# Cross-attention and mixture-of-experts kernel on one core: the split expert weights move from 192 to 64 modulo 256 bytes in SBUF

## What is computed

```
x = x + xattn(ctx_1024, layernorm(x), ...)      # 16 heads of 64, 77 context rows per batch
h = layernorm(x)
probs  = softmax(h @ Wr)                        # 9 experts, the best 2 of a token, weights rescaled to sum 1
gate   = silu(einsum('th,ehi->tei', h, Wg))     # 256 -> 704
hidden = gate * einsum('th,ehi->tei', h, Wu)    # 256 -> 704
out    = einsum('tei,eih,te->th', hidden, Wd, cw)   # 704 -> 256
x = x + out
```

## Time and profile before

| | before |
|---|---|
| median of 3 runs | 799.77 us (799.15 to 800.23) |
| profiled execution, whole | 799.43 us |
| profiled execution, span | 797.6 us |
| PE busy in the span | 769.0 us (96%) |
| PEld busy | 736.7 us (92%) |
| DVE busy | 649.1 us (81%) |
| ACT busy | 609.9 us (76%) |
| granted TensorE clock, mean | 0.991 |

### The profile page before, as it was taken

The page is one execution under the profiler, slowest core; times in us unless marked ns, Lnnn a source line. Parts: engine busy times, 40 slices in busy tenths (PEclk is TensorE's granted clock), DMA queues, the critical chain, the costliest instruction groups (busy, mean ns, idle before and its releaser), DMA issues.

```text
span 797.6 us, 19771 instructions
## 1 busy us (share of the span) xinstructions
PE 769.0 (96%) x6057; PEld 736.7 (92%) x6057; DVE 649.1 (81%) x1584; ACT 609.9 (76%) x1942; POOL 389.4 (49%) x541
## 2 busy tenths in 40 slices
PE   9988999999999999998999999999999999999994
PEld 8857999999999999897999999999999999999994
DVE  6667898898888878887878888787897878879882
ACT  4869988898889888734877778787777877778772
POOL 5603676777777766752233243333324333234343
PEclk9999999999999999998999999999999999999998
DMA  8576401401401211645574463565656656473222
GB/s 309 162 189 208 129 28 43 146 28 41 146 29 42 80 35 38 203 134 154 148 220 99 110 167 81 125 147 147 167 153 166 154 142 169 96 217 81 49 26 28
DMA packets 78212, 96.40 MB, mean 121 GB/s; under 512 B 10851, under 2 KB 65307, under 8 KB 77979
## 3 DMA queue, kind: packets, MB, share of 16 engines
q1 hardware_dynamic: 64667, 77.25, 31.1%
q0 software_dynamic: 13440, 17.90, 12.7%
HBM read 109.46 MB, written 30.23 MB: 175 GB/s over the span
## 4 chain that ended last, share of the span: by engine, by line
PE 87%; DVE 4%; POOL 3%; issue 2%; ACT 2%; SPq 1%; DVEq 1%; DMA 1%; POOLq 0%; ACTq 0%
PE banks L362 25%; PE banks L363 24%; PE banks L364 24%; PE banks L1555 4%; PE banks L1721 2%; PE banks L1410 2%; PE banks L1569 2%; SPq L640 1%; PE banks L1494 1%; PE banks L1506 1%; DVEq L1774 1%; POOL expert_in L955 1%; POOL prob L984 1%; PE banks L1530 0%; PE banks L1693 0%
## 5 line engine op out<-in xcount | busy, mean ns | idle before, releaser
L362 PE MATMUL banks<-tok_t_hi,wgt_hi 128*128 128x256 f32 x704 | 201.4, 286 | 5.6 <-issue 4.3
L1046 POOL DMA_INDIRECT result<-res,tok_id x72 | 122.5, 1702 | 162.5 <-ACT res L1305 145.0
L363 PE MATMUL banks<-tok_t_lo,wgt_hi 128*128 128x256 f32 x704 | 196.8, 280 | 0.0
L364 PE MATMUL banks<-tok_t_hi,wgt_lo 128*128 128x256 f32 x704 | 196.8, 280 | 0.0
L1170 ACT ACTIVATE prob<-banks,row_min 128x77 f32<-128x77 f32 x512 | 161.4, 373 | 4.2 <-DVE row_min L1923 4.2
L362 PEld LDWEIGHTS banks<-tok_t_hi,wgt_hi 128*128 128x128 f32 x704 | 133.8, 190 | 7.6 <-issue 7.5
L363 PEld LDWEIGHTS banks<-tok_t_lo,wgt_hi 128*128 128x128 f32 x704 | 133.5, 190 | 0.0
L364 PEld LDWEIGHTS banks<-tok_t_hi,wgt_lo 128*128 128x128 f32 x704 | 133.2, 189 | 0.0
L1170 ACT ACTIVATION_READ_ACCUMULATOR prob<-banks,row_min 128x1 f32 x512 | 130.0, 256 | 0.0
L362 PE MATMUL banks<-wgt_hi,hid_hi 128*128 128x256 f32 x360 | 101.5, 282 | 0.7 <-DVE hid_hi L2239 0.7
L984 POOL TENSOR_TENSOR prob<-prob,row_inv 128x1232 f32<-128x1232 f32 x32 | 72.1, 2253 | 59.8 <-DVE row_inv L1937 59.8
(11 more groups left out here) (280 smaller groups left out, 2173.9 us busy)
## 6 DMA issues: line engine op xcount, KB each, us to landing
wgt<-in_L_ffn_Wg SPq DMA_DIRECT2D x29, 704.0 KB
wgt<-in_L_ffn_Wu SPq DMA_DIRECT2D x29, 640.0 KB
wgt<-in_L_ffn_Wd SPq DMA_DIRECT2D x29, 640.0 KB
tok<-expert_in SPq DMA_DIRECT2D x32, 258.0 KB, 3.8
spare_wgt<-in_L_ffn_Wg SPq DMA_DIRECT2D x9, 704.0 KB, 4.6
spare_wgt<-in_L_ffn_Wu SPq DMA_DIRECT2D x9, 640.0 KB, 5.9
spare_wgt<-in_L_ffn_Wd SPq DMA_DIRECT2D x9, 640.0 KB, 6.2
valmat_f<-valmat_dram SPq DMA_DIRECT2D x4, 1197.0 KB, 6.2
```

The lines of the kernel that those rows point to most:

```text
L362: nc.tensor.matmul(to, a[0], b[0], start=first, stop=False)
L363: nc.tensor.matmul(to, a[0], b[1], start=False, stop=False)
L364: return nc.tensor.matmul(to, a[1], b[0], start=False, stop=last)
L1046: nc.gpsimd.indirect_dma_start(out, bass.IndirectOffsetOnAxis(ap=tok_id[:, t % NOTES, a:a + 1], axis=0), res[i][:, a, :], None, compute_op ...
```

## The change

Two gap tensors grow from 16 to 48 columns of 4 bytes (+128 bytes each), and the third, of 32 columns (128 bytes), is gone.

```diff
-        sb("line_gap0", [P, 16], F32, ffn)
+        sb("line_gap0", [P, 48], F32, ffn)
         wgt_hi = [sb("wgt_hi0", [P, WCOLS], F32R, ffn)]
         wgt_lo = [sb("wgt_lo0", [P, WCOLS], F32R, ffn)]
         gate_act = [sb(f"gate_act{i}", [P, 2, W], F32, ffn) for i in range(2)]
         hid_f = [sb(f"hid_f{i}", [P, 2, W], F32, ffn) for i in range(2)]
-        sb("line_gap1", [P, 16], F32, ffn)
+        sb("line_gap1", [P, 48], F32, ffn)
         hid = [[sb("hid0_hi", [P, FC, W], F32R, ffn), sb("hid0_lo", [P, FC, W], F32R, ffn)],
                [sb("hid1_hi", [P, FC, W], F32R, ffn), hid1_lo]]
         res = [sb("res0", [P, WB, D], F32, ffn), res1]
...
         wgt = sb("wgt", [P, WEIGHT_SLOTS, WCOLS], F32, ffn)
-        sb("line_gap2", [P, 32], F32, ffn)
         wgt_hi.append(sb("wgt_hi1", [P, WCOLS], F32R, ffn))
```

## The result

| | before | after |
|---|---|---|
| median of the runs | 799.90 us (798.68 to 801.06, 6 runs) | 802.53 us (801.20 to 803.27, 6 runs) |
| ratio, 95% interval | | 1.0037 (1.0026 to 1.0048) |
| span of the profiled execution | 797.6 us | 799.8 us |

The change makes the kernel slower by 0.37%, 2.6 us at the medians. The page's head after it answers to the earlier trace rows: same instructions, PE busy for 4.4 us more.

What follows compares the result with a forecast made beforehand. PE's matmul pitch in the expert stage was taken as the bound. Matmuls +2.7 us and singles -0.6, with 0.4 hidden by pauses, gave +1.7 us: a median of 801.5 us, range 795.2 to 805.6.

Steps and rivals of the forecast that it cites:

- The bound: Expert stage: its length is PE's matmuls, read from the start-to-start pitch; PE busy 408.19 of 413 us.
- Step 1, the kind: Expert stage's gate_up and down: runs still settle at 113.5 or 117.9 ns, with somewhat more slow pitch; attention unchanged.
- Step 1, the size: Gate_up and down going from +64 to -64: an even mix of fast and slow pitch, 2.7 us more.
- half price: Lower bound for gate_up and down at -64, if a single tile's price counts by half: 1.1 us more.
- full price: Upper bound for gate_up and down at -64, if a single tile's price counts in full: 6.8 us more.
- That a run's beginning counts: Gate_up and down runs: position alone does not decide the pitch; it depends also on how the run begins.
- Step 2: Single tiles going to +64: their 96 long matmuls fall from 394 to 388 ns, giving back 0.6 us.
- Steps 3 and 4: DVE and ACT reading and writing from other places, and loads and stores moved by 128 or 256 bytes: nothing.
- The pauses: PE's eight waits at tile boundaries in the expert stage: hide about a fifth of the matmuls' loss, 0.4 us.
- The fast pitch as the rule: Rival: all gate_up and down fall to 113.5 ns, 795.9 us; faster in one form or another has chance 0.33.
- No effect: Rival: gate_up and down pitch comes from how a run begins, not the distance; time stays at 799.8 us; chance 0.25.
- The slow pitch as the rule: Rival: -64 puts all gate_up and down at 117.9 ns, +7.1 us, 806.9 us; chance 0.08.

Runs made afterwards that it cites:

- e12: e9's placing of parts, but around the change's distance of -64 instead of +64 between stationary and moving operands; 798.75 us, 0.9989 against the kernel before.
- e9: Kernel before, with gate and up columns of wgt_lo and both hid_lo 128 bytes apart from their rounded parts, wgt_lo's down rows level; 796.23 us, 0.9954.
- e1: Kernel before, with tokens, split weights and hidden rows all moved by 128 bytes, so every distance stays; 800.26 us, 1.0011.
- e2: Kernel before, with split weights and hidden rows moved and tokens left: gate_up gets the change's -64, down keeps its distances; 799.33 us, 0.9992.
- e3: Kernel before, with hid0_lo moved to 128 modulo 256, apart from hid0_hi, as slot 1 has it; 799.79 us, 1.0000.
- e4: Kernel before, with hid1_lo moved from 128 to 0 modulo 256, level with hid1_hi; 800.28 us, 1.0003.
- e8: Kernel before, with tokens, split weights and hidden rows all at 128 modulo 256, so every distance is 0; 810.01 us, 1.0122.
- e5: Kernel before, with wgt_lo0 alone moved from 192 to 64 modulo 256, apart from its rounded part in slot 0; 1.0003.
- e6: Kernel before, with wgt_lo apart from wgt_hi in both slots, hid_lo level in both, and three small tables moved into gaps; 1.0003.
- e7: As e6, with both hid_lo also 128 bytes apart from their hid_hi; 804.10 us, 1.0044 against the kernel before.
- e11: Kernel before, with only tok_t_lo, gate_up's moving rest, put 128 bytes apart from tok_t_hi; 802.86 us, 1.0025.

## Why the prediction was right, and where it was not

**The bound** was right. The time moved with PE's pitch: 4.1 + 0.25 - 1.7 = 2.65 us by the count, against 2.2 us between the profiled spans and 2.6 between the medians.

**Step 1, the kind.** Right: the two pitches are still there, the attention did not answer (318.20 against 317.86 us busy, with one matmul more in the stretch), and -64 has a larger share of the slow one. e12 against e9, and the eight runs that e1 and e2 tell apart, show that this is the distance and not this one arrangement.

**Step 1, the size.** It was too small: 4.1 us instead of 2.7. I had the share go from 0.30 to an even mix of 0.50; by the starts it went from 0.39 to 0.69. Two things were off. The even mix was a choice for want of evidence; the measured 4.1 us lie about midway between its half price (1.1 us) and its full price (6.8 us). And I read the share from mean durations, which understated it before (0.28 and 0.34), and gave "means near 279.5" as the sign of the size. The mean was 279 (whole stage, line 363), as forecast, but it says little, for durations do not keep to the pitch. These are the groups of 48 gate_up matmuls at the slow pitch (388.8 to 394.1 us) and of 48 at the fast one (401 to 406 us) in the changed kernel, columns as in the earlier trace rows:

```profile
L363 PE MATMUL banks<-tok_t_hi,wgt_lo 128*128 128x256 f32 x15 | 4.2, 279 | 0.0
```

```profile
L363 PE MATMUL banks<-tok_t_hi,wgt_lo 128*128 128x256 f32 x16 | 4.4, 276 | 0.0
```

Before, the same two pitches had 282 and 277. Read on that scale, the first of them would pass for a mixture.

**That a run's beginning counts** was right, and more so than I used it. In the kernel before, slot 0's gate_up comes directly behind a slow down and is mostly fast; slot 1's comes behind a fast down and is slow half the time. When e3 made slot 0's down fast, gate_up took back what down had gained. After the change most runs begin slow and stay there.

How the pitch is handed on was not in the prediction, and the traces show it. I took the 21 gate_up runs of 48 that come directly behind a down, from 374 us on, and compared each with that down. At +64 (before, e1, e3, e4) the run takes the other pitch: 68 of 84, and 16 to 18 of 21 in each kernel. At -64 (after, e2) it takes the same pitch: 33 of 42, 16 and 17 of 21. So before, a slow down bought a fast gate_up, which gave back all of e3's gain and part of e4's loss; after, slot 0's slow down is mostly followed by a slow gate_up. No run tells why the sign turns.

**Step 2** had the wrong sign: the singles' 512-column matmuls went from 394 to 396 ns and their step from 230.5 to 233.1 ns, +0.25 us instead of -0.6. At +64 they do not have the one low level that I took for them.

```profile
L362 PE MATMUL banks<-wgt_lo,tok_t_hi 128*128 128x512 f32 x32 | 12.7, 396 | 0.0
```

**Steps 3 and 4** were right: DVE's rest 883 ns, ACT's rounding 785, by the groups of the first section.

**The pauses** took back 1.7 us, which is two fifths of the matmuls' loss and not one. The eight at tile boundaries shrink from 4.1 to 2.5 us together; in e8 the nine are down to 0.9 us, so they took back 3.9 of 15.2 us.

The misses of the terms, by the count, are +1.4 (gate_up and down), +0.85 (singles) and -1.3 us (pauses). They partly cancel and leave 0.95 us, about the difference between 801.5 and the measured 802.5. The forecast is closer than its terms are, and that is luck: the singles' wrong sign and the pauses' wrong size hid each other.

**The rivals.** *The fast pitch as the rule*: no, the slow share rose. But the clue that spoke for it, slot 1's fast down with `hid1_lo` standing otherwise, was real: it is the stationary rest 128 bytes apart that makes it fast (e3, e4), and not -64. *No effect*: excluded by e8, where placement alone takes nearly every gate_up and down matmul to 120.0 ns and the time up by 1.22%. The rule of the Trainium skill in "SBUF — State Buffer", "Who interferes with whom", that PE's port for the moving operand and its port for the weight load are independent, was weighed for that rival; the measurement decides against the conclusion drawn from it, since where the one operand stands modulo 256 relative to the other changes the pitch. *The slow pitch as the rule*: not quite, 0.69 of the steps; the 806.9 us of that case lie 4.4 us above the median.

**What stays open.** How the two reads meet is argued from positions alone; no run shows the mechanism, and none tells why the slow level is 4.4 ns above the fast one and distance 0 another 2.2. Why slot 1's gate_up rose in e1, whose distances are all kept, is not explained, nor is slot 0's down in e2 beyond the handover from run to run (in e1 that handover does not hold: behind a slow gate_up its slot 0's down is slow in 10 of 11 cases). The counts above the floor are of one profiled execution each: e2, e3, e5 and e6 lie 0.3 to 1.4 us above the kernel before in them and within 0.13% in time, with intervals as wide as that. e12 shows how far one execution can lie from its kernel's median, 2.4 us. How the slow share would look at distances that are no multiple of 64 was not tried.

## What to carry to other kernels

When PE is the bound with matmuls of this kind (float32r, 256 columns, a weight load for each), read the pitch from start to start, over the whole stage and for each kind of run, since the durations hide it and a run that gets faster in one place can hand the slow pitch to the next. Choose the positions of the operands modulo 256 bytes in pairs: for this kernel +64 between stationary and moving was best, 0 and 128 cost 5 to 6% of every such matmul, and of split operands the stationary rest belongs 128 bytes from its rounded part and the moving rest level with it. A tensor that is stationary in one product and moving in another may need both, and then its parts are placed apart, as in e9.

## What the runs showed of the hardware that was not expected

- A float32r matmul of 256 columns has several pitches at full clock with nothing waited for. With all operands at +64 or all at -64, a run of gate_up mostly settles at 113.4 or 117.8 ns and keeps it for dozens of matmuls; at distance 0 it is 120.0 nearly throughout. Elsewhere the steps vary within a run: the mean is 118.7 ns over all runs at distance 128, and 120.1 to 120.6 in a down run of e7, with steps up to 130 ns.
- At +64 a gate_up run mostly takes the opposite pitch of the down run ahead of it (68 of 84), at -64 the same one (33 of 42).
- The two roles differ: a rest 128 bytes apart gives a slow share of 0.11 to 0.20 where it is stationary and the moving one is level (down in e3 and e9, gate_up in e6 and e9), and of 0.83 to 0.88 where it is moving (down in e5's slot 0, e6 and e7, gate_up in e11), with no run at the fast pitch. That is around +64; around -64 the arrangement of e9 has 0.44 and 0.26 (e12).
- Single tiles, with the roles turned and 512 columns, hardly react: 228.9 to 233.1 ns over all kernels, 229.0 in e8 where the pair tiles are at their worst.
